# The decay matrix of a chunk on ACT: sixteen rectified differences and an exponential, in place of two GpSimd passes

## The reference, cut to what matters

```python
xn = _layernorm(x)
x = x + attn(xn) + ffn(xn)          # attn(xn) = xn + _mamba2(xn)
# _mamba2: z, xBC, dt = xn @ w_in; xBC = silu(conv(xBC)); dt = softplus(dt + dt_bias); A = -exp(A_log)
# _ssd, per chunk, 16 heads h, A_cs = cumsum(dt * A) within the chunk:
Lmat = jnp.exp(_segsum(A))          # exp(A_cs[l] - A_cs[s]) for s <= l, else 0
Y_diag = jnp.einsum('bcln,bcsn,bhcls,bcshp->bclhp', Cm, Bm, Lmat, X)
Y_off = jnp.einsum('bchpn,bcln,bhcl->bclhp', states, Cm, jnp.exp(A_cs))
# y = (Y_diag + Y_off + xh * D) * silu(z), normalized, @ w_out
# _ffn: hidden = fwht(silu(x @ W1.T) * (x @ W3.T)); out = hidden @ W2.T
```

## Time and profile before

| | |
|---|---|
| three runs | 1009.56, 1010.45 (median), 1012.27 us |
| profiled execution, its own time | 1006.74 us |
| its span | 1004.9 us |
| mean granted clock | 0.982 |
| instructions | 13326 |

### The profile page before, as it was taken

How to read it: one execution, slowest core, us unless ns; L and a number is a source line. 1 busy time by engine, 2 the same in 40 slices (tenths; PEclk the granted TensorE clock), 3 DMA queues, 4 the chain that set the end, 5 groups by cost and what they waited for, 6 DMA issues and landing times.

```text
span 1004.9 us, 13326 instructions
## 1 busy us (share of the span) xinstructions
PE 941.8 (94%) x4960; PEld 469.0 (47%) x4960; DVE 597.8 (59%) x1064; ACT 391.2 (39%) x680; POOL 264.3 (26%) x164
## 2 busy tenths in 40 slices
PE   3799779899989999999999999999999999999997
PEld 2334335444434445554544445555544445555543
DVE  5687477688633565757651666666651666666621
ACT  5576764635222334442321334442321344343200
POOL 0132343452000201645200201654400201645300
PEclk9899899999989999999999999999999999999999
DMA  9579454664422434554322434554322534355123
GB/s 330 202 263 389 154 180 142 236 199 148 157 76 82 162 96 112 168 149 118 121 65 63 170 95 115 158 157 126 105 66 61 174 95 135 92 157 147 44 74 95
DMA packets 80944, 142.65 MB, mean 142 GB/s; under 512 B 8176, under 2 KB 21104, under 8 KB 78832
## 3 DMA queue, kind: packets, MB, share of 16 engines
q1 hardware_dynamic: 61808, 113.83, 35.6%
q10 hardware_dynamic: 19072, 27.97, 9.3%
HBM read 115.82 MB, written 25.95 MB: 141 GB/s over the span
## 4 chain that ended last, share of the span: by engine, by line
PE 79%; DVE 7%; ACT 6%; issue 4%; DMA 2%; POOL 1%; SPq 0%; ACTq 0%; DVEq 0%; POOLq 0%
PE ps L541 51%; PE ps L741 16%; PE ps L706 3%; PE ps L698 2%; PE ps L692 2%; PE ps L661 1%; DVE arena L1121 1%; DMA arena<-cs_rows 1%; PE ps L678 1%; ACT arena L800 1%; DMA arena<-w_dt 1%; ACT arena L823 1%; ACT arena L956 1%; DVE arena L1142 1%; DVE wo_lo L1194 1%
## 5 line engine op out<-in xcount | busy, mean ns | idle before, releaser
L541 PE MATMUL ps<-xh,arena 128*128 128x512 f16 x1600 | 494.8, 382 | 10.9 <-DVE arena L1121 5.0
L541 PE MATMUL ps<-xl,arena 128*128 128x512 f16 x800 | 305.9, 382 | 0.0
L541 PEld LDWEIGHTS ps<-xh,arena 128*128 128x128 f16 x1600 | 159.6, 100 | 203.3 <-issue 19.4
L741 PE MATMUL ps<-arena 128*128 128x512 f16 x768 | 173.3, 382 | 0.0
L1286 POOL TENSOR_TENSOR arena<-arena 128x512 f16<-128x512 f32 x64 | 83.0, 1298 | 293.8 <-ACT arena L870 293.7
L1301 POOL TENSOR_TENSOR arena<-arena 128x2048 f32<-128x2048 f32 x16 | 58.9, 3681 | 294.5 <-DMA arena<-cs_rows 294.5
L1121 DVE SCALAR_TENSOR_TENSOR arena<-ps,cw,arena 128x511 f32<-128x511 f32 (+2 forms) x120 | 89.6, 749 | 55.8 <-ACT arena L860 53.8
L541 PEld LDWEIGHTS ps<-xl,arena 128*128 128x128 f16 x800 | 78.7, 98 | 89.7 <-issue 5.0
L741 PEld LDWEIGHTS ps<-arena 128*128 128x128 f16 x768 | 75.1, 99 | 93.5 <-issue 9.1
L870 ACT ACTIVATE arena<-arena 128x512 f16<-128x512 f32 x64 | 40.3, 630 | 168.0 <-DVE arena L1142 168.0
L541 PE MATMUL ps<-wo_hi,arena 128*128 128x512 f16 x256 | 78.7, 379 | 1.2 <-DVE arena L1249 1.2
(11 more groups left out here) (157 smaller groups left out, 1073.7 us busy)
## 6 DMA issues: line engine op xcount, KB each, us to landing
arena<-w_parts SPq DMA_DIRECT2D x198, 256.0 KB, 2.7
w_parts<-arena SPq DMA_DIRECT2D x66, 256.0 KB, 3.2
arena<-cs_rows ACTq DMA_DIRECT2D x16, 1024.0 KB, 6.0
arena<-w SPq DMA_DIRECT2D x48, 256.0 KB, 7.0
arena<-w SPq DMA_DIRECT2D x8, 1024.0 KB, 14.1
arena<-ecs_rows ACTq DMA_DIRECT2D x24, 256.0 KB, 6.9
w_mid<-arena SPq DMA_DIRECT2D x16, 256.0 KB, 2.6
arena<-x ACTq DMA_DIRECT2D x16, 256.0 KB, 4.0
```

What stands on the lines that cost most here:

```text
L541: ins = nc.tensor.matmul(out_ap, lhs(i, a), rhs(i, c), start=(i == 0 and s == 0), stop=(i == n - 1 and s == 2))
L741: ins = nc.tensor.matmul(bank(t), hw[a][:, i, t * P:(t + 1) * P], w2s[i % W2R][:, d, :], start=(i == 0 and s == 0), stop=(i == JF - 1 and ...
```

## The change

The table of places gets a step D at the counts 2, 9, 16 and 24 of A/U tiles. POOL's part of the step E goes away. ACT's part of D waits for what POOL waited for, makes in 16 instructions of 128x128, one per head, relu(cs_s - csbc), which is the negated and clamped difference, waits for them (`erelu_ok`), and takes exp(-value) in one instruction of 128x2048. ACT's part of X goes away with its wait for the clamp. The loads of `csbc` (L931) and of the half-transformed W2 (L505) wait for `erelu_ok` in place of `esub_ok`. The lists become `Z7 D0 T0 ...`, `A4 D1 U4`, `U7 R1 D2 N1 Q1 A8` and `U11 R2 D3 N2 Q2 A12`; in batch 0, where T0 comes earlier, `U0 F2 WOQ2 WOQ3 D0 A1` and `A4 WOH4 WOH5 D1 U4`.

```diff
     "E": (None, 6, 14, 22),
+    "D": (2, 9, 16, 24),
     "Y": (6, 14, 22, 32),
...
                     elif kind == "HL":
-                        sp.wait_ge(esub_ok.sem, esub_ok.at(0, NC - 1))
+                        sp.wait_ge(erelu_ok.sem, erelu_ok.at(0, NC - 1))
...
-                        act.wait_ge(esub_ok.sem, esub_ok.at(b, c - 1))
+                        act.wait_ge(erelu_ok.sem, erelu_ok.at(b, c - 1))
...
-                    elif kind == "X":
-                        act.wait_ge(emin_ok.sem, emin_ok.at(b, c))
-                        nc.scalar.activation(Eb, Eb, ACT.Exp).then_inc(eexp_ok.sem, 1)
+                    elif kind == "D":
+                        act.wait_ge(d_csbc, (b * NC + (c + 1)) * 16)
+                        act.wait_ge(sums_ok.sem, sums_ok.at(b, 0))
+                        act.wait_ge(pe_diag.sem, pe_diag.at(b, c - 1))
+                        for h in range(NH):
+                            ins = nc.scalar.activation(Eb[:, h, :], csbc[:, h, :], ACT.Relu, bias=cs_s[:, c * NH + h:c * NH + h + 1],
+                                                       scale=-1.0)
+                        ins.then_inc(erelu_ok.sem, 1)
+                        act.wait_ge(erelu_ok.sem, erelu_ok.at(b, c))
+                        nc.scalar.activation(Eb, Eb, ACT.Exp, scale=-1.0).then_inc(eexp_ok.sem, 1)
...
-                    elif kind == "E":
-                        pool.wait_ge(d_csbc, (b * NC + (c + 1)) * 16)
-                        pool.wait_ge(sums_ok.sem, sums_ok.at(b, 0))
-                        pool.wait_ge(pe_diag.sem, pe_diag.at(b, c - 1))
-
-                        nc.gpsimd.tensor_tensor(Eb, csbc, cs_s[:, c * NH:(c + 1) * NH].unsqueeze(2).to_broadcast([P, NH, P]),
-                                                ALU.subtract).then_inc(esub_ok.sem, 1)
-                        pool.wait_ge(esub_ok.sem, esub_ok.at(b, c))
-                        nc.gpsimd.tensor_tensor(pool_mark[:], ones[:, 0:1], ones[:, 0:1], ALU.mult)
-                        nc.gpsimd.tensor_scalar(Eb, Eb, 0.0, -3.0e38, ALU.min, ALU.max).then_inc(emin_ok.sem, 1)
```

More of the change, by code:

```diff
@@ L356, in build @@
         xdec_ok = signal("xdec_ok", NC - 1)
-        esub_ok = signal("esub_ok", NC, 1)
-        emin_ok = signal("emin_ok", NC)
+        erelu_ok = signal("erelu_ok", NC, 1)
         eexp_ok = signal("eexp_ok", NC)
```

## The result

The changed kernel takes 1048.7 us (median of 4 runs, 1048.1 to 1049.8), the kernel before 1010.9 (4 runs). The ratio is 1.038, with a 95% interval of 1.036 to 1.040. The forecast was 1049, in a range of 1029 to 1066. The profiled execution took 1048.1 us with a span of 1046.3, 41.4 more than the span before.

A forecast was written before the change was run, and what follows sets the result against it. PE was taken as the bound in batches 1 to 3. Losses of 22.3 us there, 13.6 in batch 0 and 3 for the clock, 38.9 in sum, on the median 1010.45 gave 1049 us, range 1029 to 1066.

The forecast's parts named there:

- Reading of the bound: In batches 1 to 3 PE is the bound, POOL and ACT cost it nothing, and any new PE stall adds in full.
- The block D: 6.8 us: On ACT, sixteen relus 4.8 us, wait 0.1 and exponential 1.90; no activation table load.
- The walks: Batch 2 followed chunk by chunk for PE's losses: D0 1.9, D1 0, D2 2.2, D3 3.9, sum 8.0 us.
- W1 late by the same 2 us and not more: Batch 2 behind D2: W1 needs V1, late on DVE by as much as D2's loss, with no further loss.
- Batches 1 and 3: Same list as batch 2, only the load's landing differs: batch 1 loses 7.6 us, batch 3 loses 6.7.
- Batch 0: 13.6: Four D blocks in batch 0 at 3.4 us each, 13.6 in all; bounds 2 and 4.9 per block.
- The clock: one fall, 3 us: One PE stall lowers the granted clock to half, costing 3 us; bounds 0 and 12.
- the prediction's own sign: Forecast wrong if batch 2's PE idle grows under 4 us, or clock is 0.5 in over two stretches behind 130 us.
- the rival "faster": POOL off DVE's back in batch 0 and batch 1, ACT's block covered: 6 us less, 1004; chance 5%.
- Half: Batch 0's stalls vanish in its idle 23 us, only batches 1 to 3 lose: 1032; chance 11%.
- relus don't overlap: Sixteen relus on ACT take 6.3 us, 1.5 more at 12 to 16 blocks: 1070; chance 5%.
- Clock falls at each D3 and D2: Four to five more falls of PE's clock at 3 us each: 1062; chance 13%.

The follow-up runs named there:

- the moved kernel: Changed kernel with D2 and D3 put behind the tanh of A9 and of A13, and X2 at 20: 1010.0 us, ratio 1.002 to the kernel before.
- the doubled D1 and D3: Two runs of the changed kernel, one chunk's relus done twice in batches 1 to 3: chunk 1 1049.7 us, ratio 1.041; chunk 3 1064.4 us, ratio 1.055.

## Why the prediction was right, point by point

**Reading of the bound.** Right in the main. PE was the bound of batches 1 to 3, and the loss came from where D stands, as the moved kernel and the doubled D1 and D3 show. But "nothing that POOL or ACT does costs PE anything today" was wrong: of the 2.7 us in which PE is idle in batch 2, 1.6 are the wait in the front that POOL causes.

**The block D: 6.8 us.** Measured 6.71. No table load. Both as taken.

**Batch 2.** The walks' own times give 1.8, 2.0 and 3.8 us where the text has 1.9, 2.2 and 3.9, 0.4 less in all. D0 1.9, measured 1.7; D1 0, measured 0. D2 2.2: the wait before U9 was 2.3. But "W1 late by the same 2 us and not more" was wrong: PE waited another 1.2 us there. X2 and the remainder of y (L1246, then L1253) on DVE, before and after, up to the read of the mean (L1249, then L1256) for which W1 waits:

```profile
674.16 3.16 DVE L1207 TENSOR_TENSOR arena<-arena 128x2048 f32<-128x2048 f32 x1 [2.54 <-ACT arena L956]
677.24 2.18 DVE L1246 SCALAR_TENSOR_TENSOR arena<-arena 128x1024 f16<-128x1024 f32 x1
679.34 0.15 DVE L1249 TENSOR_SCALAR arena<-ps 128x1 f32<-128x1 f32 x1
...
698.69 0.68 DVE L1149 SCALAR_TENSOR_TENSOR arena<-ps,arena 128x512 f32<-128x512 f32 x1
699.29 3.42 DVE L1214 TENSOR_TENSOR arena<-arena 128x2048 f32<-128x2048 f32 x1
702.63 2.17 DVE L1253 SCALAR_TENSOR_TENSOR arena<-arena 128x1024 f16<-128x1024 f32 x1
704.73 0.14 DVE L1256 TENSOR_SCALAR arena<-ps 128x1 f32<-128x1 f32 x1
```

X2 starts 25.1 us later than before, where everything ahead of D2 was 21.6 later: 3.5 us, not 2.2, since the pass over A8, T2's two operations and the pass over U8 (L1149) now stand in one line in front of it. W1 had no slack for the difference: before, it started 0.3 us behind the start of L1249. Both X2 and the remainder are slower than their 2.29 and 1.28 us elsewhere, but they were before too, and so this isn't the cause. Both stand beside POOL's passes, before and after:

```profile
673.27 1.90 POOL L1309 TENSOR_TENSOR arena<-arena 128x1024 f32<-128x1024 f32 x1
675.13 3.21 POOL L1286 TENSOR_TENSOR arena<-arena 128x512 f16<-128x512 f32 x1
...
698.66 1.91 POOL L1306 TENSOR_TENSOR arena<-arena 128x1024 f32<-128x1024 f32 x1 [10.01 <-DVE arena L1205]
700.52 3.20 POOL L1293 TENSOR_TENSOR arena<-arena 128x512 f16<-128x512 f32 x1
```

D3 3.9: the wait was 4.0.

**Batches 1 and 3.** D0 as in batch 2. D2 2.4 and 1.5 were forecast, 1.4 and 2.25 measured without the clock: the load of chunk 2, on which they hang, took 6.0 us and not 9.6 in batch 1, and 8.6 in batch 3, where 5.0 was its time in the trace before. D3 3.3 each, measured 3.3 and 3.6.

**Batch 0: 13.6, measured 14.9.** The sum held; the division didn't. "3.4 for each" was wrong: D0 cost 0.4, since PE's idle stretch with its half clock was there before and only moved, and D1 and D3 cost 4.9 and 5.8, at and above my upper bound of 4.9. That bound left out that a longer stall can also lower the clock. The forecast had no fall for batch 0, since "there PE waits for ACT anyway"; PE's busy time there (up to 294.9 us before, 309.8 after) grew from 246.7 to 250.0 us with the same matmuls. So the stalls were some 11.6 us and not 13.6, and the sum held since the clock made up for it.

**The clock: one fall, 3 us.** This term was mis-sized: the falls in batches 1 to 3 took 1.7 + 1.85 + 2.6 + 1.4 = 7.6 us. The step that failed is "The stalls foreseen in batches 1 to 3 reach 3.9 us, just under that", with one fall put in for all. The row it rests on the earlier trace rows spoke against it: the granted clock of the stall of 4.3 us is already 0.91, so the level fell before that stall was over. By the prediction's own sign, 0.5 in more than two stretches behind 130 us, this part was wrong: the changed kernel has nine such stretches and the kernel before two, beside the last 1.4 and 1.6 us of each. A stall of 3.3 us in batch 1 was followed by the lower level, and of two stalls at the same place, 2.3 us in batch 2 and 2.25 in batch 3, only the second was. Stretches of the changed kernel on PE (busy us, then the granted clock), idle and behind it, for batch 2 and for batch 3:

```profile
695.30:697.60 2.30, 0.01 (x1) 1.00 0.49 154
697.60:700.00 2.40, 2.40 (x12) 1.00 0.00 0
930.00:932.10 2.10, 0.00 (x0) 1.00 0.50 135
932.10:934.00 1.90, 1.87 (x5) 0.55 0.02 5
```

**What the sum left out: POOL off DVE's back outside batch 0.** I costed POOL's removed passes at nothing in batches 1 to 3, since nobody waited for POOL. That is not the same as nobody being held by it. The fronts gave 5.1 us. The prediction cites the very rule, but only for the rival "faster" and for batch 0. DVE's L1103, at a mean of 890 ns in the kernel before and 700 in the changed one, would have told; I read the timeline only around the D steps.

**Why the total is close.** The clock took 4.6 us more than forecast and V1 1.2, batch 0 1.3; the fronts gave 5.1 that weren't in the sum. Misses of opposite sign cancel in 1049 against 1048.7, and in batch 0 another two did; the difference of the two spans, 41.4, stands 2.5 over the sum of 38.9. The mechanism and the stalls that I worked out for batches 1 to 3 are right; that the total is within a microsecond is luck.

**The rivals.** "Faster" was priced on a true mechanism, at 6 us, and it is 11 to 14, but D's places rule it out. "Half" and "relus don't overlap" are refuted by the table and the 4.78 us. "Clock falls at each D3 and D2" is half true: four of six, at 1.9 us each on average and not 3; three more fell in batch 0, at D1, D2 and D3.

What stays open: which stalls lower the clock. I have three cases with a fall at 3.3 to 4.0 us, and two stalls of one length that differ, and made no run on it. The doubled kernels add one more such pair: a stall of 2.0 us before U9 with the lower level behind it (batch 2, D3 twice), and one of 2.0 us without (batch 3, D1 twice).

## What to carry to other kernels

Where engines walk one list in order, the cost of an operation is its length less the slack at its place: with the same relus on ACT the kernel was 38 us slower than before at one set of places, 2 us slower at another, and 7 us faster when they were cut up and spread over other places. Before moving a step to an idle engine, list what stands behind it on that engine and when the bound engine wants each of these. And when an operation is taken away, look not only for who waits for it but for who is slow beside it: compare the minimum and the mean of the other engines' groups.

## What was not expected of the hardware

A POOL pass of 3.6 us stretched a DVE pass of 0.68 us to between 3.3 and 3.6, in the front of each of the batches 1 to 3, with no semaphore between them; in the page this looks like DVE work and not like a wait. After a PE stall of only 2.3 us the granted clock of the next stretch was once 1.00 and once 0.55, and the second cost 1.85 us, nearly as much again as the stall itself.
